# Moving a row copy, splitting the first loads and placing the decay products elsewhere in a linear-attention and mixture-of-experts kernel

## The chip, the cores and the metric

The kernel runs on one core of a Trainium2 chip. The metric is the device time of one execution in microseconds. TensorE (PE in the profile) multiplies, VectorE (DVE), ScalarE (ACT) and GpSimd (POOL) work beside it, and SyncE (SP) issues most of the transfers. POOL and ACT have transfer queues of their own. Engines meet only at semaphores, and each engine takes its instructions strictly in order.

## The reference

The input is layer-normalised once; the output is the input plus an attention branch plus an expert branch.

```
xn  = layernorm(x)                            # x: 1024 tokens x 256
q, k, v = split(xn @ w_qkv);  q, k = elu(.)+1
decay = sigmoid(decay_param)                  # one value for each of 16 heads
kv_t = decay*kv_(t-1) + k_t*v_t;  ks_t = decay*ks_(t-1) + k_t
attn = (q * kv / max(sum_d(q * ks), 1e-6)) @ w_out
e = argmax(xn @ router_w.T);  gate = sigmoid(max logit)
routed = (silu(g) * u) @ w_down[e],  [g, u] = (xn*gate) @ w_gate_up[e]   # 8 experts, top 1
shared = (silu(g') * u') @ shared_down, [g', u'] = xn @ shared_gate_up
out = x + attn + routed + shared
```

## The kernel before

**Tiles.** The 1024 tokens are eight tiles of 128 (`NT`), in two halves of four (`TH` = 4). The work is written out by hand: one list of instructions for each engine, with waits on semaphores between them.

**Start.** SP issues two loads of x with two tiles each, the k part of w_qkv, and, once the second load of x has landed, the v part, the other two loads of x and the q part. ACT issues the small loads of the router and of `decay_param`. PE runs 14 matmuls on constants (L985) in this time, then transposes the router (L989). DVE takes the statistics of the first four tiles (`statistics`, L600), then aggregates all four (L604). ACT takes the root (L451), DVE makes 1/root more exact (L613 to L618) and normalises three tiles (L620); ACT normalises the fourth (L439). PE transposes them (L855), ACT rounds the result to `xT_hi` (L444), and DVE forms the rest, `xT_lo` (`x_lo`, L626), from which the third pair of matmuls of the first projection tile reads (`hi_lo`, L914). The second half follows the same way. `root_eps` is a square root of a constant (L449), which brings the table of square roots into ACT before it is wanted.

**Decay.** After the root of the second half, ACT forms exp(-decay_param) (L466). DVE forms 1/(1+that) after the second `normalise` (L692, L693). PE spreads the 16 values over 128 partitions with two small products (L1006) between projection tiles 6 and 7, and DVE copies the result to `decay` (L733) late in the projection. The scans over tokens read `decay`.

**Middle.** PE runs 12 projection tiles (`qkv_tile`, in PSUM banks 0 to 3 in turn), the router, and seven of the eight shared gate/up tiles. DVE, ACT and POOL place each token in a row of `sorted_rows` in HBM, grouped by expert in tiles of 144 rows.

**Expert tiles.** Eight tiles (t = 0 to 7 here), one for each expert. On PE a tile is: the gate/up products of half 0 (16 matmuls, L1040), the transposes that bring the result of tile t-1 back to rows (`transpose_back`, L979), the gate/up products of half 1, the transposes of the input of tile t+1 (L971), and the down products (L1054), of which the first 8 read the half-0 result of DVE and the last 8 the half-1 result. For each half ACT takes the silu (L541) and DVE multiplies (L793, `hr`). DVE also copies the transposed rows of tile t-1 from PSUM to the one buffer `yrow` (`rows_copy`, L788), and POOL stores `yrow` to `sorted_rows` (L418). Before the copy DVE waits until PE has transposed and until the store before has landed, as `yrow` is one buffer:

```
def rows_copy(t):
    dve.wait_ge(s_yback, t + 1)
    dve.wait_ge(s_ystore, 16 * t + 16)
    V.tensor_copy(yrow[...], ps[0:HS, 7, :]).then_inc(s_yrow, 1)
```

PE in turn waits in `transpose_back(t + 1)` of the next tile for that copy (`s_yrow`), as the rows lie in one PSUM bank. SP refills the expert weights, 1 MB (`gu`, L339) after the gate/up products of a tile and 0.5 MB (`dn`, L341) after its down products, for the expert two further on.

**End.** A ninth `rows_copy` and store (L420) bring the last tile home. When all stores have landed, POOL gathers the eight token tiles (L427). Meanwhile PE runs the last shared tile, the shared down products and the attention output into eight PSUM banks. DVE adds the gathered rows (L834) and the PSUM result (L838); in its order the sum with tile i-4 from PSUM stands behind the sum with gathered tile i. SP stores each finished tile (L359).

Of the kernel before, what the change touches and what calls it, by code (L numbers as in the profile page):

```python
# [13 lines left out]
P = 128  # L14
# [9 lines left out]
def build(nc, x, w_qkv, w_out, decay_param, router_w, w_gate_up, w_down, shared_gate_up, shared_down, out):  # L24
# [23 lines left out]
    with ExitStack() as ctx:  # L48
# [12 lines left out]
        root_eps = sb("root_eps", [P, 1], F32)  # L61
        head_of = sb("head_of", [P, KC, HEADS], F32)
# [116 lines left out]
        s_x = [sem(f"s_x{n}") for n in range(2 * NH)]  # L179
# [113 lines left out]
        def _(sp):  # L293
            def x_load(n):
                two = slice(2 * n, 2 * n + 2)
                sp.dma_start(x_sb[:, two, :], x_rows[:, two, :]).then_inc(s_x[n], 16)
# [5 lines left out]
            x_load(0)  # L302
            x_load(1)
            w_load(1, s_wk)
            sp.wait_ge(s_x[1], 16)
# [127 lines left out]
        def _(act):  # L433
# [11 lines left out]

            act.dma_start(router[:, :], router_w).then_inc(s_router, 16)
            act.dma_start(dec_in[:, :], decay_param.rearrange("(h o) -> h o", o=1)).then_inc(s_dec, 16)
# [17 lines left out]
            act.wait_ge(s_dec, 16)  # L465
            A(dec_e[:, :], dec_in[:, :], ACT.Exp, scale=-1.0).then_inc(s_dece, 1)  # L466
# [112 lines left out]
        def _(dve):  # L579
# [16 lines left out]
            def statistics(i):  # L596

                if i % 2 == 0:
                    dve.wait_ge(s_x[i // 2], 16)
                return V.bn_stats(bn[:, i, :], x_sb[:, i, :])  # L600

            def variances(n):
                for i in range(n * TH, (n + 1) * TH):
                    ins = V.bn_aggr(mv[:, i, :], bn[:, i, :])  # L604
# [66 lines left out]
            for i in range(TH):  # L671
                ins = statistics(i)
            link(ins)
            variances(0)
            normalise(0)
            dve.wait_ge(s_whk, 1)
# [3 lines left out]
            x_lo(0)  # L680
            dve.wait_ge(s_rhi, 1)
# [7 lines left out]
            variances(1)  # L689
            normalise(1)  # L690
            dve.wait_ge(s_dece, 1)
            link(V.tensor_scalar(dec_1[:, :], dec_e[:, :], 1.0, None, ALU.add))  # L692
            V.reciprocal(dec_h[:, :], dec_1[:, :]).then_inc(s_dech, 1)  # L693
# [19 lines left out]
            for a in range(2 * NH):  # L713
# [14 lines left out]
                if a == KC:  # L728
# [3 lines left out]
                    dve.wait_ge(s_decp, 1)  # L732
                    V.tensor_copy(decay[:, :], ps[:, 7, 256:256 + KC]).then_inc(s_decay, 1)  # L733
# [56 lines left out]
            def expert_tile(t):  # L790
                for h in range(2):
# [3 lines left out]
                    if h == 0:  # L795
                        rows_copy(t)
# [44 lines left out]
        def _(pe):  # L841
# [46 lines left out]
            def qkv_tile(t):  # L888
# [7 lines left out]
                if t:  # L896
                    pe.wait_ge(s_xlo, 2 * n + 2)
                if t >= 4:
# [92 lines left out]
            transpose_tokens(0)  # L991
            for t in range(3):
# [121 lines left out]
```

## Time and profile before

| | |
|---|---|
| median of 3 runs | 133.34 us (132.67 to 134.13) |
| the profiled execution | 133.63 us |
| its span, first to last instruction | 132.0 us |
| granted TensorE clock | 1.00 of full |
| PE busy | 125.1 us (95%) |
| DVE, ACT, POOL busy | 79.1, 52.7, 30.9 us |
| chain that ended last | PE 58%, DMA 26%, DVE 7%, ACT 3%, issue 3% |

The span is what the traces show; the execution's time has 1.6 us more around it. The page gives shares over the whole span, the timeline the start and length of single instructions, the windows the sums of a stretch, and the chain what released what.

### The profile page before, as it was taken

What the parts mean: (1) busy time and instruction counts of PE and PEld (TensorE: products, weight loads), DVE (VectorE), ACT (ScalarE), POOL (GpSimd) and SP (SyncE); (2) the same over time, 40 slices, a digit from 0 to 9 for tenths busy, and PEclk for the clock granted to TensorE, in tenths of its full rate; (3) what the DMA queues carried; (4) which work ended last, traced back from release to release, by engine and by line L of the source; (5) the groups of instructions that cost most, each with busy time, mean ns of one, the idle gap of its engine ahead of it and who ended that gap; (6) DMA issues with size and microseconds to landing.
All of it is one profiled execution on the core that took longest, in us unless ns stands there. A gap on an engine that the chain in (4) does not pass through costs nothing.

```text
span 132.0 us, 2426 instructions
## 1 busy us (share of the span) xinstructions
PE 125.1 (95%) x830; PEld 108.3 (82%) x830; DVE 79.1 (60%) x161; ACT 52.7 (40%) x104; POOL 30.9 (23%) x55
## 2 busy tenths in 40 slices
PE   4989989999999999999999999999798999999992
PEld 1247757788888885999999988999697997999991
DVE  0699886989999998455286447401917512413472
ACT  3265796869965956422222221313252223100000
POOL 7704000027786000020202002020202021177600
DMA  2684999999942101029899999999992120123364
GB/s 81 210 267 103 307 354 211 236 376 406 409 181 104 45 0 50 20 60 310 266 296 281 370 394 337 352 349 360 307 353 78 45 69 28 45 82 97 102 195 168
DMA packets 20052, 27.40 MB, mean 208 GB/s; under 512 B 1336, under 2 KB 16864, under 8 KB 20040
## 3 DMA queue, kind: packets, MB, share of 16 engines
q1 hardware_dynamic: 14152, 21.43, 50.2%
q0 software_dynamic: 1408, 3.58, 8.5%
q10 hardware_dynamic: 4480, 2.24, 5.8%
q8 instruction: 7, 0.11, 0.3%
q14 instruction: 5, 0.04, 0.1%
HBM read 19.90 MB, written 7.34 MB: 206 GB/s over the span
## 4 chain that ended last, share of the span: by engine, by line
PE 58%; DMA 26%; DVE 7%; issue 3%; ACT 3%; ACTq 0%; POOLq 0%; DVEq 0%
DMA sorted_rows<-yrow 19%; PE ps L288 10%; PE ps L290 10%; PE ps L289 10%; PE ps L1040 6%; DMA den<-den_rows 5%; PE ps L908 5%; PE ps L1054 4%; PE ps L921 4%; PE ps L914 4%; DMA x_sb<-in_L_attn_x_dram 2%; DVE yrow L788 2%; ACT xT_hi L444 1%; DVE bn L600 1%; PE ps L855 1%
## 5 line engine op out<-in xcount | busy, mean ns | idle before, releaser
L1040 PE MATMUL ps<-xgT,gu 128*128 128x144 f32 x256 | 34.2, 287 | 0.1
L1040 PEld LDWEIGHTS ps<-xgT,gu 128*128 128x128 f32 x256 | 32.4, 190 | 0.7 <-issue 0.5
L1054 PE MATMUL ps<-wqkv,dn 128*128 128x144 f32 x128 | 18.2, 292 | 1.5 <-DVE wqkv L793 1.5
L418 POOL DMA_DIRECT2D sorted_rows<-yrow x8 | 5.6, 699 | 59.6 <-DVE yrow L788 59.6
L1054 PEld LDWEIGHTS ps<-wqkv,dn 128*128 128x128 f32 x128 | 16.3, 190 | 2.2 <-DVE wqkv L793 2.2
L793 DVE TENSOR_TENSOR wqkv<-rz,ps 128x288 f32<-128x288 f32 x16 | 7.2, 451 | 17.4 <-ACT rz L541 17.4
L541 ACT ACTIVATE rz<-ps 128x288 f32<-128x288 f32 x16 | 6.6, 410 | 26.4 <-PE ps L1040 26.4
L288 PE MATMUL ps<-xT_hi,sgu_hi 128*128 128x512 f32 x32 | 12.8, 399 | 0.0
L289 PE MATMUL ps<-xT_lo,sgu_hi 128*128 128x512 f32 x32 | 12.5, 391 | 0.0
L290 PE MATMUL ps<-xT_hi,sgu_lo 128*128 128x512 f32 x32 | 12.5, 390 | 0.0
L788 DVE COPY yrow<-ps 72x512 f32<-72x512 f32 x9 | 6.1, 683 | 10.1 <-DMA sorted_rows<-yrow 7.4
L410 POOL DMA_INDIRECT sorted_rows<-xn,slot_row x8 | 9.8, 1231 | 3.7 <-ACT xn L475 2.1
L544 ACT ACTIVATE yT<-ps 128x288 f32<-128x288 f32 x8 | 3.3, 410 | 14.8 <-PE ps L1054 14.8
L289 PE MATMUL ps<-wqkv_lo,hT_hi 128*128 128x256 f32 x32 | 9.1, 283 | 0.0
L288 PE MATMUL ps<-wqkv_hi,hT_hi 128*128 128x256 f32 x32 | 9.1, 283 | 0.0
L290 PE MATMUL ps<-wqkv_hi,hT_lo 128*128 128x256 f32 x32 | 9.0, 281 | 0.0
L908 PE MATMUL ps<-xT_hi,wqkv_hi 128*128 128x512 f32 x24 | 8.2, 419 | 0.7 <-DVE ksum L716 0.4
L427 POOL DMA_INDIRECT q_sb<-sorted_rows,slot_row x8 | 7.7, 964 | 4.9 <-POOLq L423 2.7
L834 DVE TENSOR_TENSOR x_sb<-x_sb,q_sb 128x256 f32<-128x256 f32 x8 | 3.4, 424 | 7.4 <-DMA q_sb<-sorted_rows,slot_row 7.4
L921 PE MATMUL ps<-xT_hi,wqkv_lo 128*128 128x512 f32 x24 | 7.6, 397 | 0.0
L914 PE MATMUL ps<-xT_lo,wqkv_hi 128*128 128x512 f32 x24 | 7.5, 396 | 0.0
L985 PE MATMUL ps<-ones 128*128 128x512 bf16 x14 | 5.5, 495 | 1.8 <-POOL ones L367 1.8
(153 smaller groups left out, 227.7 us busy)
## 6 DMA issues: line engine op xcount, KB each, us to landing
gu<-in_L_ffn_w_gate_up_dram SPq DMA_DIRECT2D x8, 1024.0 KB, 7.5
dn<-in_L_ffn_w_down_dram SPq DMA_DIRECT2D x8, 512.0 KB, 8.4
sorted_rows<-zeros SPq DMA_DIRECT2D x1, 2592.0 KB, 16.6
sorted_rows<-yrow POOLq DMA_DIRECT2D x10, 144.0 KB, 4.8
wqkv<-sorted_rows SPq DMA_DIRECT2D x10, 144.0 KB
x_sb<-in_L_attn_x_dram SPq DMA_DIRECT2D x4, 256.0 KB, 3.2
sgu<-_ffn_shared_gate_up_dram SPq DMA_DIRECT2D x1, 1024.0 KB, 6.1
rden_rows<-rden ACTq DMA_DIRECT2D x1, 1024.0 KB, 14.0
```

The costliest lines, as they stand in the source:

```text
L288: nc.tensor.matmul(o, w_hi, m_hi, start=start, stop=False)
L289: nc.tensor.matmul(o, w_hi, m_lo, start=False, stop=False)
L290: return nc.tensor.matmul(o, w_lo, m_hi, start=False, stop=stop)
L410: pool.indirect_dma_start(sorted_rows, bass.IndirectOffsetOnAxis(ap=slot_row[:, i:i + 1], axis=0), xn[:, i, :], None).then_inc(s_scatter, 16)
L427: pool.indirect_dma_start(y_tok[:, i, :], None, sorted_rows, bass.IndirectOffsetOnAxis(ap=slot_row[:, i:i + 1], axis=0)).then_inc(s_gather ...
L788: V.tensor_copy(yrow[:, :, :].rearrange("p j d -> p (j d)"), ps[0:HS, 7, :]).then_inc(s_yrow, 1)
L793: V.tensor_tensor(hr[:, 2 * h:2 * h + 2, :].rearrange("p f s -> p (f s)"), act_sb[:, h, 0:2 * SLOTS], ps[:, 2 * h + 1, 0:2 * SLOTS], ALU.m ...
L908: mm(o, wqkv_hi[:, kc, cols], xT_hi[:, kc, rows], start=(kc == 0), stop=False)
L914: ins = mm(o, wqkv_hi[:, kc, cols], xT_lo[:, kc, rows], start=False, stop=last and kc == KC - 1)
L921: ins = mm(o, wqkv_lo[:, kc, cols], xT_hi[:, kc, rows], start=False, stop=last and kc == KC - 1)
L1040: ins = mm(ps[:, 2 * h + u, (f % 2) * SLOTS:(f % 2 + 1) * SLOTS], gu[p][:, kc, col:col + P], xgT[:, kc, :], start=(kc == 0), stop=(kc == K ...
L1054: ins = mm(ps[:, 5 + c, 0:SLOTS], dn[p][:, f, c * P:(c + 1) * P], hr[:, f, :], start=(f == 0), stop=(f == FC - 1))
```

## The change

Three edits go together.

1. In an expert tile DVE does `rows_copy(t)` after both products L793 instead of between them. There is still one buffer `yrow`.
2. The first four tiles of x come in four loads of one tile, tiles 0 and 2 from SP, tiles 1 and 3 from ACT's queue, with a semaphore for each; `decay_param` is loaded between ACT's two and the router after them. DVE waits for each tile and aggregates a tile's statistics one tile later.
3. exp(-decay_param) becomes ACT's first activation, ahead of `root_eps`. A new `exp_eps` (an exp of a constant) stands where the exp stood. DVE's two decay operations come right after the first `normalise`, PE's two small products right after the first transposes (into bank 3), the copy to `decay` after the first `x_lo`. Projection tile 3 waits for that copy.

```diff
-            x_load(0)
-            x_load(1)
+            for i in range(0, TH, 2):
+                sp.dma_start(x_sb[:, i, :], x_rows[:, i, :]).then_inc(s_xt[i], 16)
             w_load(1, s_wk)
-            sp.wait_ge(s_x[1], 16)
+            sp.wait_ge(s_xt[TH - 2], 16)
+            sp.wait_ge(s_xt[TH - 1], 16)
...
+            act.dma_start(x_sb[:, 1, :], x_rows[:, 1, :]).then_inc(s_xt[1], 16)
+            act.dma_start(dec_in[:, :], decay_param.rearrange("(h o) -> h o", o=1)).then_inc(s_dec, 16)
+            act.dma_start(x_sb[:, 3, :], x_rows[:, 3, :]).then_inc(s_xt[3], 16)
             act.dma_start(router[:, :], router_w).then_inc(s_router, 16)
-            act.dma_start(dec_in[:, :], decay_param.rearrange("(h o) -> h o", o=1)).then_inc(s_dec, 16)
+            act.wait_ge(s_dec, 16)
+            A(dec_e[:, :], dec_in[:, :], ACT.Exp, scale=-1.0).then_inc(s_dece, 1)
             act.wait_ge(s_const, 1)
             A(root_eps[:, :], eps[:, :], ACT.Sqrt)
...
-            act.wait_ge(s_dec, 16)
-            A(dec_e[:, :], dec_in[:, :], ACT.Exp, scale=-1.0).then_inc(s_dece, 1)
+            A(exp_eps[:, :], eps[:, :], ACT.Exp)
...
             for i in range(TH):
-                ins = statistics(i)
-            link(ins)
-            variances(0)
+                here = mark(statistics(i))
+                if i:
+                    need(last)
+                    aggregate(i - 1)
+                last = here
+            need(last)
+            variances(0, [TH - 1])
             normalise(0)
+            dve.wait_ge(s_dece, 1)
+            link(V.tensor_scalar(dec_1[:, :], dec_e[:, :], 1.0, None, ALU.add))
+            V.reciprocal(dec_h[:, :], dec_1[:, :]).then_inc(s_dech, 1)
...
             x_lo(0)
+            dve.wait_ge(s_decp, 1)
+            V.tensor_copy(decay[:, :], ps[:, 3, 0:KC]).then_inc(s_decay, 1)
...
             normalise(1)
-            dve.wait_ge(s_dece, 1)
-            link(V.tensor_scalar(dec_1[:, :], dec_e[:, :], 1.0, None, ALU.add))
-            V.reciprocal(dec_h[:, :], dec_1[:, :]).then_inc(s_dech, 1)
...
-                    dve.wait_ge(s_decp, 1)
-                    V.tensor_copy(decay[:, :], ps[:, 7, 256:256 + KC]).then_inc(s_decay, 1)
...
-                    if h == 0:
-                        rows_copy(t)
+                rows_copy(t)
...
+                if t == 3:
+                    pe.wait_ge(s_decay, 1)
...
             transpose_tokens(0)
+            pe.wait_ge(s_dech, 1)
+            for c in range(KC):
+                ins = mm(ps[:, 3, c:c + 1], spread[:, c, :], dec_h[:, :], start=True, stop=True)
+            ins.then_inc(s_decp, 1)
...
             ranks()
-            pe.wait_ge(s_dech, 1)
-            for c in range(KC):
-                ins = mm(ps[:, 7, 256 + c:257 + c], spread[:, c, :], dec_h[:, :], start=True, stop=True)
-            ins.then_inc(s_decp, 1)
```

## Rows read from the trace of the kernel before

**Rows 1.** The page, busy time of each engine and its share of the span.

```profile
PE 125.1 (95%) x830; PEld 108.3 (82%) x830; DVE 79.1 (60%) x161; ACT 52.7 (40%) x104; POOL 30.9 (23%) x55
```

**Rows 2.** Windows, one expert tile each (1, 3, 5, 6): length, then busy us by engine.

```profile
59.33:65.95 6.62, 6.62 (x58) 6.61 (x57) 2.59 (x4) 1.53 (x4) 0.72 (x1) 1.00 0.89 288
...
72.69:80.27 7.58, 7.21 (x57) 6.72 (x57) 3.97 (x6) 1.65 (x5) 0.68 (x1) 1.00 1.08 371
...
87.01:94.70 7.69, 6.89 (x58) 6.66 (x57) 2.64 (x5) 1.53 (x4) 0.68 (x1) 1.00 1.02 331
94.70:102.08 7.38, 6.90 (x59) 6.68 (x58) 3.78 (x6) 3.31 (x6) 0.69 (x1) 1.00 0.68 246
```

**Rows 3.** Timeline of expert tiles 1 and 5: start, length, instruction, [idle before <-releaser].

```profile
61.29 0.60 PE L979 MATMUL ps<-ident,yT 128*72 128x128 f32 x4
...
62.31 0.68 DVE L788 COPY yrow<-ps 72x512 f32<-72x512 f32 x1
...
64.33 0.46 DVE L793 TENSOR_TENSOR wqkv<-rz,ps 128x288 f32<-128x288 f32 x1 [1.35 <-ACT rz L541]
...
92.52 0.69 DVE L788 COPY yrow<-ps 72x512 f32<-72x512 f32 x1 [2.45 <-DMA sorted_rows<-yrow]
...
93.62 0.76 PE L1054 MATMUL ps<-wqkv,dn 128*128 128x144 f32 x4 [0.80 <-DVE wqkv L793]
```

**Rows 4.** The chain that ended last: row stores 2 to 5, from issue to landing.

```profile
70.56 7.13 DMA sorted_rows<-yrow
...
79.20 5.53 DMA sorted_rows<-yrow
...
86.24 6.18 DMA sorted_rows<-yrow
...
93.94 5.86 DMA sorted_rows<-yrow
```

**Rows 5.** DMA issues at 57.16, 71.55 and 106.47 us; last column: us to landing.

```profile
sorted_rows<-yrow POOLq DMA_DIRECT2D x1, 144.0 KB, 3.0
...
gu<-in_L_ffn_w_gate_up_dram SPq DMA_DIRECT2D x1, 1024.0 KB, 8.5
...
sorted_rows<-yrow POOLq DMA_DIRECT2D x1, 144.0 KB, 2.8
```

**Rows 6.** Timeline of the end: ninth copy, first gather, last sums, last output store.

```profile
110.19 0.69 DVE L788 COPY yrow<-ps 72x512 f32<-72x512 f32 x1 [2.65 <-PE ps L979]
...
115.01 1.04 POOL L427 DMA_INDIRECT q_sb<-sorted_rows,slot_row  x1 [2.73 <-POOLq L423]
...
126.76 0.43 DVE L834 TENSOR_TENSOR x_sb<-x_sb,q_sb 128x256 f32<-128x256 f32 x1 [0.49 <-DMA q_sb<-sorted_rows,slot_row]
127.10 0.74 DVE L838 TENSOR_TENSOR x_sb<-x_sb,ps 128x256 f32<-128x256 f32 x2
...
129.44 0.42 DVE L838 TENSOR_TENSOR x_sb<-x_sb,ps 128x256 f32<-128x256 f32 x1 [0.29 <-PE ps L290]
...
129.89 0.33 SPq L359 DMA_DIRECT2D out_dram<-x_sb  x1
```

**Rows 7.** Timeline of the start: ACT's second load, table load, root_eps, first root.

```profile
1.60 0.34 ACTq L447 DMA_DIRECT2D dec_in<-_L_attn_decay_param_dram  x1
...
1.98 1.28 ACT L449 ACT_TABLE_LOAD   x1 [1.98 <-issue]
...
3.27 0.20 ACT L449 ACTIVATE root_eps<-eps 128x1 f32<-128x1 f32 x1
...
5.97 0.30 ACT L451 ACTIVATE sd<-mv,eps 128x4 f32<-128x4 f32 x1 [2.50 <-DVE mv L604]
```

**Rows 8.** Timeline: PE's wait in projection tile 0; DVE's second decay operation.

```profile
10.73 0.19 PEld L914 LDWEIGHTS ps<-xT_lo,wqkv_hi 128*128 128x128 f32 x1 [0.17 <-DVE xT_lo L626]
...
14.83 0.15 DVE L693 RECIPROCAL dec_h<-dec 16x1 f32<-16x1 f32 x1
```

**Rows 9.** The chain that ended last: PE's small decay products (start, us).

```profile
23.85 0.53 PE ps L1006 x4
```

More of the change, by code:

```diff
@@ L61, in build @@
         root_eps = sb("root_eps", [P, 1], F32)
+        exp_eps = sb("exp_eps", [P, 1], F32)
         head_of = sb("head_of", [P, KC, HEADS], F32)
@@ L176, in build @@
         count_ps = ps[:, ROUTE, 192:192 + NT * E]
-        s_x = [sem(f"s_x{n}") for n in range(2 * NH)]
+        s_xt = [sem(f"s_xt{i}") for i in range(TH)]
+        s_x = [sem(f"s_x{n}") for n in range(TH // 2, 2 * NH)]
         s_router = sem("s_router")
@@ L295, in x_load @@
                 two = slice(2 * n, 2 * n + 2)
-                sp.dma_start(x_sb[:, two, :], x_rows[:, two, :]).then_inc(s_x[n], 16)
+                sp.dma_start(x_sb[:, two, :], x_rows[:, two, :]).then_inc(s_x[n - TH // 2], 16)
             def w_load(j, s_w):
@@ L596, in statistics, with aggregate, variances @@
             def statistics(i):
-                if i % 2 == 0:
-                    dve.wait_ge(s_x[i // 2], 16)
+                if i < TH:
+                    dve.wait_ge(s_xt[i], 16)
+                elif i % 2 == 0:
+                    dve.wait_ge(s_x[(i - TH) // 2], 16)
                 return V.bn_stats(bn[:, i, :], x_sb[:, i, :])
-            def variances(n):
-                for i in range(n * TH, (n + 1) * TH):
-                    ins = V.bn_aggr(mv[:, i, :], bn[:, i, :])
+            def aggregate(i):
+                return V.bn_aggr(mv[:, i, :], bn[:, i, :])
+            def variances(n, tiles):
+                for i in tiles:
+                    ins = aggregate(i)
                 ins.then_inc(s_var, 1)
@@ L688, in _ @@
             link(ins)
-            variances(1)
+            variances(1, range(TH, NT))
             normalise(1)
-            dve.wait_ge(s_dece, 1)
-            link(V.tensor_scalar(dec_1[:, :], dec_e[:, :], 1.0, None, ALU.add))
-            V.reciprocal(dec_h[:, :], dec_1[:, :]).then_inc(s_dech, 1)
             dve.wait_ge(s_wlk, 1)
```

## The prediction

> **What bounds the kernel now.** I read the page first: PE is busy for 95% of the span [rows 1]. So there is little idle PE time to win, and the question is where PE waits. The chain of work next: between projection and the last sum it runs through PE, except in the expert stage, where it runs through the stores of `yrow` [rows 4]. That is a warning and not yet a price, since a chain names what came last, not by how much. The windows, cut at the start of each expert tile, give the price: an undisturbed tile takes 6.62 us, tiles 3, 5 and 6 take 7.58, 7.69 and 7.38 [rows 2], which is 0.96 + 1.07 + 0.76 = 2.79 us over. The timeline of tile 5 shows how: DVE stands 2.45 us before the copy, waiting for the store, and the half-1 product behind it comes late, so that PE waits 0.80 us between its two halves of down products [rows 3]. The start and the end are the other places where PE isn't the only engine on the path.
>
> **Edit 1, the copy behind both products.** In this order the store no longer stands in front of the half-1 product. The loop itself stays: copy, 1.42 us until the store is issued (92.52 to 93.94), landing, some 0.1 us, next copy [rows 3, 4]. Its period is 1.42 + landing + 0.1; the four landings of 7.13, 5.53, 6.18 and 5.86 us [rows 4] give 8.65, 7.05, 7.70 and 7.38, mean 7.69, more than a tile's 6.62. What changes is the slack. The half-1 product starts 5.00 us into a tile (59.33 to 64.33), so an undelayed copy starts at 5.0 + 0.37 = 5.37 us instead of 62.31 - 59.33 = 2.98 [rows 2, 3]; 0.37 is the distance from product to copy that tile 1 shows. The next to need it is PE's transpose back, 1.96 us into the next tile (61.29) [rows 3]; the copy must start 0.76 us before it, at 7.8 us. So the loop may fall behind by 2.4 us before PE waits, but it starts 2.4 us later and is bound by the store from tile 0 on, not from tile 2.
>
> The first copy comes at 52.7 + 5.37 = 58.1 (tile 0 begins one tile of 6.62 before 59.33). With p the mean of six periods (stores 0 to 5) the seventh copy starts at 58.1 + 6p, tile 7's transpose back 0.76 later, and the stage ends 6.62 - 1.96 = 4.66 after that: 58.1 + 6p + 5.4. It ended at 108.6, one undisturbed tile after 102.08 [rows 2]. PE's own limit: in tile 3 the wait hides another one. The 1 MB refill issued at 71.55 lands after 8.5 us, at 80.05 [rows 5], and tile 4 begins at 80.27, the end of tile 3 [rows 2]. So tile 3's 0.96 stays, and at most 1.07 + 0.76 = 1.83 us can go.
>
> What are the periods? Store 0 now follows the refill of `gu` instead of preceding it; preceding it, it landed in 3.0 us [rows 5]. The nearest row for a store behind a refill with little else in flight is 5.86 (period 7.38) [rows 4]; the bounds are 3.0 and 7.13. I take five periods of 7.5 and a sixth of 6.5, because by then the refills run out (after them a store landed in 2.8 us [rows 5]): 58.1 + 37.5 + 6.5 + 5.4 = 107.5, a gain of **1.1 us**. With 7.38 throughout it is 107.8 (0.8 gained); with 7.4 five times and 6.5 it is 107.0, close to the limit of 1.83; with 7.69 throughout it is 109.6, a loss of 1.0.
>
> Then the end, where the price is firmer. Before, the ninth copy (110.19) waited for PE's transposes [rows 6] because store 7 had been issued at 106.47 and had landed after 2.8 us, at 109.3 [rows 5]. Copy 7 now comes 2.4 us later within its tile, so store 7 is issued at 108.9 and lands at 111.7 on the old scale: the ninth copy is 1.5 us later against PE. POOL's eight gathers stand behind the ninth store, the first at 115.01, and move with it. The sum with the last gathered tile, at 126.76, moves to 128.3. Behind it in DVE's queue stand the PSUM sums of tiles 3 to 7. Two of them took 0.74 us with 0.42 for one, so they follow each other by 0.32 [rows 6]: the last starts near 128.3 + 0.35 + 4 x 0.33 = 130.0 instead of 129.44, 0.55 later. Their output stores are then issued back to back by SP at 0.33 us each [rows 6] and about 0.1 between, 0.43 x 4 after a first at 129.1: the last at 130.8 instead of 129.89. I take **0.9 us lost**, bounds 0.5 and 1.5. DVE's `hidden(LAST)` also stands behind the ninth copy; it moves by 0.3 us, and PE has two shared-down tiles ahead of its need.
>
> Other work behind the moved copy on DVE, the scans, `sdn_lo` and the attention products, moves by up to 2.4 us. Only in tile 4 does it get near a product (q times kv and `wout_lo`, 3 us after copy 3); worth 0 to 0.5 us, which the range holds.
>
> **Edit 2, four loads.** Statistics start when the first 256 KB have landed, and the root follows at 5.97 [rows 7]. Half the size for tile 0 and aggregation between the tiles would let the root start some 0.2 to 0.4 us earlier: three of the four aggregations leave the path. But ACT is in the way. Its four issues (0.34 us for the small one [rows 7], about 0.5 for each of x) end near 2.8; a table load of 1.28 us follows and ends at 4.1. The exp waits for `decay_param`, issued at 1.6 and now between loads of x: between 4.2 and 4.6. After it comes the second table load of 1.28, and `root_eps`, 0.2 [rows 7]: the root can run at 5.9 to 6.2. Before, one table load ended at 3.26, long before it was needed. So the earlier statistics meet a busier ACT: **0.1 us lost**, bounds 0.3 gained and 0.3 lost. SP's wait for tile 3 moves the v weights and the later x loads by up to 0.4 us. They are covered, since the v part is first rounded after `x_hi(0)`.
>
> The Trainium skill ("ScalarE: Activation LUTs", the section on table sets and the one on what a table load costs) says to batch activations by set and not to alternate exp and sqrt, and prices each switch at about 1.28 us of load plus 1.38 us of drain. That speaks against this edit, which adds one switch. The trace agrees on the load; the drain doesn't show, as `root_eps` starts at 3.27, right at the end of the load [rows 7]. By the page's 2.66 us a switch the root would stand near 2.8 + 2.66 + 0.2 + 2.66 + 0.2 = 8.5, an estimate from that page.
>
> **Edit 3, the decay products.** They leave PE's dense stretch, where they cost 0.53 us [rows 9]: a gain of 0.5, since tile 7's banks are free by then. They enter between the first transposes and projection tile 0, where PE waits for ACT's `xT_hi`. No row bounds that but the two extremes, 0 (all under the wait) and 0.53 (none); I take 0.15, near the first, as PE has nothing else there. DVE's two operations of 0.15 [rows 8] enter before `w_lo` and `x_lo`. That is no idle gap on DVE: PE already waits 0.17 us for `xT_lo` in tile 0 [rows 8], so their 0.3 us goes straight through. The two delays overlap, since tile 0 waits for both in turn: 0.3 in all. DVE's copy of 0.15 before the router's remainder has slack until the router's products. Leaving the second `normalise` they free nothing that PE waits for. Sum: 0.5 - 0.3 = **0.2 us gained**, bounds 0.5 gained and 0.1 lost.
>
> **The sum.** On the profiled execution: 133.63 - 1.1 + 0.9 + 0.1 - 0.2 = 133.3. The median of the runs is 0.3 below that execution, so 133.34 - 0.3 = 133.0. A measurement of this kernel can tell about 1%, 1.3 us, from no change.
>
> **The rivals.**
>
> A. The store loop is never late (chance 0.22). If stores behind the refill land in 3 to 5 us, like store 0, then p is under 7.1, PE loses only the refill wait, and 1.83 goes. Less traffic ahead of the refills could bring these forward too and free the 0.96 of tile 3, 2.8 in all. With 0.6 at the end instead of 0.9 and the start on the good side (0.3 gained in place of 0.1 lost) that is 133.34 - 1.83 - 0.2 - 0.3 + 0.6 = 131.6, down to 130.7. For it: 3.0 us in [rows 5]. Against it: every store in [rows 4] that was issued near a refill took 5.5 us or more.
>
> B. The loop overtakes PE (0.18). One mechanism: the transpose back of tile t+1 waits for copy t, which waits for store t-1. It decides above p = (108.6 - 63.5)/6 = 7.52. At the mean of before, 7.69, the stage is 1.0 us longer, and with the end the time is 133.34 + 1.0 + 0.9 + 0.1 - 0.2 = 135.1. For it: two of the four periods before are above 7.52, and the loop is now bound two tiles earlier, with the 1 MB reciprocal store still in flight. Against it: that traffic was what made 7.13.
>
> C. Table loads hold the root (0.06). If the load for the exp started only after `decay_param` has landed (4.3), two loads would end at 7.1 and the root stand 1.2 us later: 133.0 + 1.2 = 134.2. The page of the Trainium skill named above would make it 2.5 and 135.5, an estimate. For it: nothing in [rows 7] orders load and wait. Against it: the load before began at 1.98, right after the issues.
>
> **How the numbers follow.** My forecast, a small gain inside the noise, has 0.54; its own range is 132.1 to 134.2. A reaches down to 130.7, B up to 135.1 and beyond. A range of 131.4 to 135.1 leaves out about 0.2. Faster by over 1% means under 132.0: most of A, 0.21. Slower means over 134.7: B, part of C and a bad end, 0.22. The rest is 0.57.
>
> **What would show each step.** Tile windows: 3 stays near 7.5, 5 and 6 fall to 6.6 to 7.0. PE's waits move from the down products to L979, if any. Copies stand 5.4 to 7.8 us into their tiles. The ninth copy is released by the store, not by PE; the gathers start 1.5 us later against PE's last shared tile; the last output stores go out back to back. At the start two table loads precede the first root, which stands within 0.3 us of 5.97. The gap before L914 in tile 0 grows by 0.2 to 0.3. The prediction is wrong if the mean period lies outside 7.1 to 7.6, or if ACT's start order costs more than its loads.

## The result, and the profile after

The changed kernel takes 137.5 us (median of 6 runs, 136.6 to 139.1); the kernel before took 133.0 us beside it (6 runs, 132.3 to 134.1). The ratio is 1.033, interval 1.026 to 1.040: by it the change is 4.4 us slower, where 0.3 us faster was forecast and the range ended at 135.1. Ratios, here and below, are of executions within about 1.5% of the fastest of their kernel, so that edit 3 alone rests on 4 of 12 executions, the buffers with edit 3 on 6 of 12 and the attention run on 3 of 6, and the profiles of edit 3 alone and of the attention run are of executions that their ratios leave out.

The profiled execution of the changed kernel took 137.72 us with a span of 136.1, 4.1 more than before. Its granted clock was 0.993 over the whole; it was 1.00 up to the end of the expert stage and 0.96 behind it, where PE's last product is nevertheless where it was (below). So the clock doesn't explain the loss.

The windows, cut at the starts of expert tiles 1, 3, 5 and 6 as in [rows 2] (length, busy us by engine, clock, DMA share, GB/s):

```profile
59.36:65.98 6.62, 6.62 (x58) 6.61 (x57) 2.58 (x4) 1.53 (x4) 0.77 (x1) 1.00 0.86 289
72.61:80.27 7.66, 6.85 (x58) 6.64 (x57) 3.81 (x5) 1.53 (x4) 0.69 (x1) 1.00 1.04 353
87.82:95.95 8.13, 6.81 (x58) 6.60 (x57) 1.50 (x3) 1.53 (x4) 0.69 (x1) 1.00 1.00 312
95.95:104.26 8.31, 7.02 (x58) 6.67 (x57) 3.77 (x5) 3.42 (x6) 0.68 (x1) 1.00 0.70 237
```

The stage begins at 52.74, 0.03 later than before. Tile 5 takes 8.13 for 7.69 and tile 6 8.31 for 7.38; tile 4 takes 7.55 where it took 6.74. The last tile begins at 104.26 and, at 6.62, the stage ends at 110.9 instead of 108.7. So 2.2 us of the 4.1 are lost inside the stage, and 1.9 behind it.

The chain that ended last (start, us, piece) says through what. Before, it ran through four stores [rows 4]; now it enters the store loop at the first copy and leaves it only after the fifth store, through two other engines:

```profile
58.11 0.69 DVE yrow L803
...
59.58 6.64 DMA sorted_rows<-yrow
...
67.75 6.95 DMA sorted_rows<-yrow
...
76.21 5.48 DMA sorted_rows<-yrow
...
83.20 7.22 DMA sorted_rows<-yrow
...
91.93 5.29 DMA sorted_rows<-yrow
...
97.92 2.36 DVE kvsum L834 x2
100.30 1.06 ACT att_hi L577
101.36 0.31 ACT rz L547
101.69 0.47 DVE wqkv L808
```

From 58.11 to the copy at 97.31 there is no slack: the loop sets the pace of five tiles. The timeline shows where PE feels it:

```profile
75.54 0.63 PE L995 MATMUL ps<-ident,yT 128*72 128x128 f32 x4 [0.81 <-DVE yrow L803]
...
85.75 2.23 PE L1070 MATMUL ps<-wqkv,dn 128*128 128x144 f32 x16 [0.39 <-DVE wqkv L808]
...
90.51 0.69 DVE L803 COPY yrow<-ps 72x512 f32<-72x512 f32 x1 [4.45 <-DMA sorted_rows<-yrow]
...
91.26 0.63 PE L995 MATMUL ps<-ident,yT 128*72 128x128 f32 x4 [1.32 <-DVE yrow L803]
...
97.31 0.69 DVE L803 COPY yrow<-ps 72x512 f32<-72x512 f32 x1 [2.53 <-DMA sorted_rows<-yrow]
...
99.17 2.19 ACT L577 ACTIVATE att_hi<-kvsum 128x1024 fp32r<-128x1024 f32 x2 [2.60 <-DVE kvsum L834]
...
102.20 2.23 PE L1070 MATMUL ps<-wqkv,dn 128*128 128x144 f32 x16 [1.29 <-DVE wqkv L808]
```

PE no longer waits between its two halves of down products for a product caught behind the copy [rows 3]; it waits in the transposes back for the copy itself (L995). Two waits have another reason: work that stands on DVE behind the late copy. In tile 4 the scan's product and `wout_lo` stand between copy 3 and the expert products, and PE waits 0.39 us ahead of its down products. In tile 6 it waits 1.29 us: the two attention products (L834) stand on DVE behind copy 5, ACT's `att_hi` (L577) waits for them, and ACT's silu of tile 6 stands behind `att_hi`.

The end, against [rows 6]:

```profile
113.77 0.69 DVE L803 COPY yrow<-ps 72x512 f32<-72x512 f32 x1 [3.46 <-DMA sorted_rows<-yrow]
...
118.63 1.04 POOL L430 DMA_INDIRECT q_sb<-sorted_rows,slot_row  x1 [2.76 <-POOLq L426]
...
131.22 0.42 DVE L848 TENSOR_TENSOR x_sb<-x_sb,q_sb 128x256 f32<-128x256 f32 x1 [1.39 <-DMA q_sb<-sorted_rows,slot_row]
...
131.89 1.40 DVE L852 TENSOR_TENSOR x_sb<-x_sb,ps 128x256 f32<-128x256 f32 x4
...
132.00 2.29 SPq L362 DMA_DIRECT2D out_dram<-x_sb  x5
```

Counted from the end of the stage, the ninth copy is 1.4 us later (2.9 for 1.5), the first gather 1.4 (7.75 for 6.3), the sum with the last gathered tile 2.3 (20.3 for 18.1), and SP's last store ends 1.9 later (23.4 for 21.5). PE's last product is where it was, 20.4 us behind the stage, in both. Before, the last sum still waited for PE, 0.29 us [rows 6]; now the last sums stand behind the last gather.

The start, against [rows 7, 8]:

```profile
1.88 0.44 ACTq L451 DMA_DIRECT2D x_sb<-in_L_attn_x_dram  x1
...
3.00 1.28 ACT L454 ACT_TABLE_LOAD   x1 [3.00 <-issue]
4.30 0.20 ACT L454 ACTIVATE dec_e<-dec_in 16x1 f32<-16x1 f32 x1
4.51 1.28 ACT L456 ACT_TABLE_LOAD   x1
5.81 0.20 ACT L456 ACTIVATE root_eps<-eps 128x1 f32<-128x1 f32 x1
6.38 0.30 ACT L458 ACTIVATE sd<-mv,eps 128x4 f32<-128x4 f32 x1 [0.37 <-DVE mv L611]
...
5.70 0.43 DVE L608 BATCH_NORM_STATS2 bn<-x_sb 128x6 f32<-128x256 f32 x1 [1.04 <-DMA x_sb<-in_L_attn_x_dram]
...
11.37 0.19 PEld L930 LDWEIGHTS ps<-xT_lo,wqkv_hi 128*128 128x128 f32 x1 [0.40 <-DVE xT_lo L637]
```

The root is 0.41 us late, and what released it was not the second table load (over at 5.79, `root_eps` over at 6.01) but the statistics of tile 3, whose load was the last of the four to be issued, by ACT at 1.88. With DVE's two decay operations in front as well, PE comes 0.64 us late to its transposes of the second half; the dense stretch gives 0.53 back, as PE's small products have left it. So the stage begins only 0.03 us later.

### The profile page after: what moved, and what is told of

Its sections match the earlier page's. It is cut to its first block, busy times and chain, and to the rows that moved or that the text cites. A ratio compares the mean times of both kernels' runs of the same rounds, so it can differ in the third digit from the quotient of the medians.

```text
span 136.1 us, 2432 instructions
## 1 busy us (share of the span) xinstructions
PE 125.5 (92%) x830; PEld 108.1 (79%) x830; DVE 78.6 (58%) x161; ACT 54.3 (40%) x106; POOL 32.1 (24%) x55
## 4 chain that ended last, share of the span: by engine, by line
PE 43%; DMA 30%; issue 8%; DVE 7%; POOL 5%; ACT 3%; DVEq 1%; POOLq 1%
DMA sorted_rows<-yrow 27%; PE ps L1056 6%; PE ps L290 5%; PE ps L291 5%; PE ps L292 5%; PE ps L1001 5%; POOL q_sb L430 4%; PE ps L924 4%; PE ps L930 4%; PE ps L937 4%; DVE yrow L803 4%; DMA q_sb<-sorted_rows,slot_row 3%; DVE kvsum L834 2%; PE ps L1070 2%; PE ps L869 1%
## 5 line engine op out<-in xcount | busy, mean ns | idle before, releaser
L1070 PE MATMUL ps<-wqkv,dn 128*128 128x144 f32 x128 | 17.5, 290 | 1.7 <-DVE wqkv L808 1.7
L413 POOL DMA_INDIRECT sorted_rows<-xn,slot_row x8 | 11.3, 1407 | 2.8 <-issue 1.8
L1001 PE MATMUL ps<-ones 128*128 128x512 bf16 x14 | 6.2, 627 | 1.8 <-POOL ones L370 1.8
L995 PE MATMUL ps<-ident,yT 128*72 128x128 f32 x36 | 5.5, 276 | 2.3 <-DVE yrow L803 2.1
```

What stands on the lines that cost most here:

```text
L413: pool.indirect_dma_start(sorted_rows, bass.IndirectOffsetOnAxis(ap=slot_row[:, i:i + 1], axis=0), xn[:, i, :], None).then_inc(s_scatter, 16)
L1001: mm(ps[:, 0, :], ones[:, :], ones[:, :].unsqueeze(1).broadcast_to([P, 4, P]), start=True, stop=True)
L1070: ins = mm(ps[:, 5 + c, 0:SLOTS], dn[p][:, f, c * P:(c + 1) * P], hr[:, f, :], start=(f == 0), stop=(f == FC - 1))
```

## The experiments

Each was timed in turns with the kernel before on the same chip. They ran in four sessions on four chips, in which the kernel before took 134.5 to 135.2 us (medians), against 133.0 when the change was measured; the whole change wasn't timed again. So 1% is 1.35 us, and differences between rows of different sessions are less sure than the rows.

| | ratio to the kernel before | interval |
|---|---|---|
| whole change | 1.033 | 1.026 to 1.040 |
| edit 1 alone | 1.017 | 1.007 to 1.027 |
| edits 2 and 3 | 1.011 | 1.003 to 1.018 |
| edit 2 alone | 1.011 | 1.005 to 1.018 |
| edit 3 alone | 0.996 | 0.990 to 1.002 |
| change, four row buffers | 1.001 | 0.997 to 1.006 |
| before, four row buffers | 0.995 | 0.992 to 0.999 |
| before once more (control) | 1.003 | 0.999 to 1.008 |
| change, attention products first | 1.011 | 1.004 to 1.019 |
| change, no refills | 0.994 | 0.990 to 0.998 |
| before, no refills | 0.984 | 0.979 to 0.989 |
| before, buffers and edit 3 | 0.996 | 0.992 to 1.001 |
| edit 2 alone, tile 3 first | 1.002 | 0.998 to 1.006 |
| copy behind in the last tile alone | 1.010 | 1.004 to 1.017 |
| change, tile 3 first | 1.039 | 1.032 to 1.046 |
| before, buffers, edit 2 with tile 3 first | 0.989 | 0.984 to 0.995 |

**Which edit loses.** Edit 1 alone:

```
-                    if h == 0:
-                        rows_copy(t)
+                rows_copy(t)
```

> The kernel before with edit 1 alone: the row copy behind both products, the start untouched. Theory S (the loop of copy, store and next copy overtakes PE, and the copy drags what stands behind it on DVE): nearly all of the loss is here, 136.5 to 137.5 us; tiles 3 to 6 take 7.5 to 8.3 us, the mean of the six copy periods is near 7.7, the gathers start 3.5 us later than before. Rival T (the new start, or the lower granted clock, makes the loss): 133 to 133.5 us.

and the other two without it (the copy back between the products):

> The changed kernel with the row copy back between the two products, so edits 2 and 3 alone. Theory S: 133.0 us within 0.7, the expert stage begins within 0.1 us of the kernel before because the root that is 0.4 us later and the decay products taken out of the dense stretch cancel; tiles 3, 5 and 6 over 7.3 us again with PE waiting in the down products. Rival T: 136 to 137 us.

They give 1.7% and 1.1%, together 2.8% against the 3.3% of the whole, which the intervals allow. Edit 1 alone lost somewhat less than was expected (136.5 to 137.5 us would be 2.4 to 3.1%), and edits 2 and 3 lost where both theories were wrong: S had no loss, T had all of it. Nor does their profile show the 1.1%: the stage begins at 52.86 and ends at 108.8, against 52.71 and 108.7 before.

In the profile of edit 1 alone copies 0 to 6 run from 57.9 to 102.3, a mean period of 7.40, and the last tile begins at 101.87 (102.08 before). The ninth copy now waits for the store, and in tile 6 PE waits by way of the attention products as in the whole change:

```profile
99.80 2.23 PE L1053 MATMUL ps<-wqkv,dn 128*128 128x144 f32 x16 [1.08 <-DVE wqkv L793]
...
111.15 0.69 DVE L788 COPY yrow<-ps 72x512 f32<-72x512 f32 x1 [3.23 <-DMA sorted_rows<-yrow]
```

At 7.40 the forecast's formula has the stage end at 57.9 + 44.4 + 5.4 = 107.7, a stage 0.8 us shorter than before; it ends at 108.5 and is as long as before (56.0 us). Copy 6 was 0.75 us early for tile 7, so it wasn't the loop that set the start of the last tile here, but the wait in tile 6. The period differs from execution to execution (7.40 here, 7.70 in the change), and even at 7.40 the stage gains nothing. This profile (135.7 us) was the second shortest of four runs; one profile isn't the median.

**Is it the single buffer?** The row buffer was replaced by four (two in turn for tiles 0 to 6, one for tile 7, one for the last copy; seven transfers of 4 bytes ahead of the stage keep a semaphore's count):

```
-        yrow = sb("yrow", [HS, 2, D], F32)
+        yrow = [sb(f"yrow{b}", [HS, 2, D], F32) for b in range(4)]
...
+                    if t >= 2:
+                        dve.wait_ge(s_yalt[b], 16 * (t // 2))
```

In the changed kernel:

> The changed kernel with four row buffers: the first seven tiles alternate between two, the eighth and the ninth copy have one each, so a copy waits for the store two tiles before or for none. Seven one-word transfers from POOL ahead of the stage keep the semaphore counts. Theory S: no copy waits for a store, no PE wait before the transposes back, tile windows 6.6 to 6.8 except at most 0.4 to 0.9 where a refill of weights lands late, the ninth copy is released by PE again, 130.3 to 131.5 us. Rival D (the delay comes from DVE work standing behind a copy that is in any case 2.4 us later in its tile): tiles 4 and 6 stay at 7.3 us or more, 132.5 us or more.

and in the kernel before:

> The kernel before (copy between the products, old start) with the same four row buffers. Theory S: its three long tiles lose their waits, except what the late refill leaves in tile 3: 130.5 to 131.5 us, within 0.6 of the same buffers with the copy behind. If the refills of weights were the real bound, tiles 3 and 5 would stay above 7.2 and the time above 132.

In both no copy waits for a store any more, and the last tiles begin at 100.75 and 100.17. The loss of the change falls from 3.3% to 0.1%: what edit 1 loses needs the single buffer. In neither does PE wait for a product of DVE in the stage, so rival D falls as well. Both runs were expected some 2% faster than the kernel before and weren't: the second gains half a per cent, less than the 1.8 us that its waits for the copy seemed to be worth. PE waits for loads instead (timeline, before with four buffers):

```profile
77.58 0.47 PE L992 MATMUL ps<-ident,wqkv 72*128 72x72 f32 x4 [0.68 <-DMA wqkv<-sorted_rows]
```

and the refill of `gu` issued at 71.36 lands after 8.6 us, at 79.96, ahead of a tile 4 that begins at 80.22: the wait that [rows 2, 5] had shown for tile 3.

**Is it the refills?** SP's refills were left out in both orders, so that experts 2 to 7 work with the weights of experts 0 and 1 and the routed part of the result is another one:

```
-                sp.wait_ge(s_gup, 2 * done)
-                sp.dma_start(gu[p][:, :, :], gu_dram[e + 2]).then_inc(s_gu[p], 16)
-                sp.wait_ge(s_down, done)
-                sp.dma_start(dn[p][:, :, :], dn_dram[e + 2]).then_inc(s_dn[p], 16)
```

> The changed kernel without the refills of the expert weights (experts 2 to 7 work with the weights of experts 0 and 1; that part of the result is another one). Theory (the landing of the 144 KB stores under 1.5 MB refills is what makes the loop late): stores land in 2.6 to 3.5 us, a period is about 4.5 us and never binds, no copy before the eighth waits for a store, all tiles take 6.62 us, the stage ends near 105.7. Only the end stays: the ninth copy waits for store 7 (about 108.6) and stands 1.3 us later than in the kernel before without refills. Together with 0.1 to 0.3 at the start the time is 1.0 to 1.6 us above that kernel. Rival (the late copy itself costs in the stage, whatever the transfers do): tiles above 6.62 us remain.

> The kernel before without the refills of the expert weights, left out as in the run beside it. All eight tiles take 6.62 us, no copy waits for its store, the stage ends near 105.7 instead of 108.6 to 109.0, and the time is about 2.9 us under the kernel before, ratio 0.975 to 0.985. If the ratio stays above 0.99, the transfers weren't what held the stage.

All tiles of both kernels take 6.62 us. The windows of tile 5, first of the change, then of before, with a DMA share of 0.15 and 0.17 instead of 1.0:

```profile
85.81:92.44 6.63, 6.63 (x59) 6.62 (x58) 2.08 (x4) 1.54 (x4) 0.69 (x1) 1.00 0.15 44
```

```profile
85.58:92.20 6.62, 6.62 (x58) 6.61 (x57) 2.67 (x5) 1.53 (x4) 0.68 (x1) 1.00 0.17 47
```

The refills cost the kernel before 1.6% (2.2 us) and the changed one 3.9% (1.033 against 0.994, of different sessions; 5.2 us). About two thirds of the change's loss hang on them. The rival, that the late copy costs in the stage whatever the transfers do, falls: with copies that wait for no store the work behind them holds up nothing either. What is left, 1.1% or 1.4 us, is put down to the end and the start (0.23 us between the stage's starts, 52.70 and 52.47); the end is seen in the last copy of each, the change first:

```profile
108.40 0.69 DVE L799 COPY yrow<-ps 72x512 f32<-72x512 f32 x1 [3.29 <-DMA sorted_rows<-yrow]
```

```profile
106.93 0.69 DVE L784 COPY yrow<-ps 72x512 f32<-72x512 f32 x1 [2.65 <-PE ps L975]
```

**The end by itself.** The copy stands behind both products in the last tile alone:

```
-                    if h == 0:
+                    if h == 0 and isinstance(t, int):
                         rows_copy(t)
+                if not isinstance(t, int):
+                    rows_copy(t)
```

(the last tile runs in a loop with a counter in a register; the others have t as a number).

> The kernel before with the row copy behind both products in the last expert tile alone, all others as before. It measures the forecast's end term by itself. Forecast: copy 7 comes 2.4 us later, store 7 is issued near 108.9 to 109.3 and lands 2.8 us later, the ninth copy is released by that store 1.5 us later than by PE before, the eight gathers move with it, the last five sums go back to back; 0.5 to 1.5 us longer, ratio 1.004 to 1.011. Rival (the end has slack, and the whole loss is in the stage): ratio 1.000 to 1.003, and the gathers later by the same 1.5 us without the last store moving.

It costs 1.4 us, 0.5 to 2.3. Its timeline has the forecast's mechanism: the copy 5.37 us into the tile, the ninth released by the store, the gather behind it.

```profile
107.45 0.68 DVE L788 COPY yrow<-ps 72x512 f32<-72x512 f32 x1
111.50 0.69 DVE L788 COPY yrow<-ps 72x512 f32<-72x512 f32 x1 [3.37 <-DMA sorted_rows<-yrow]
...
116.33 1.04 POOL L427 DMA_INDIRECT q_sb<-sorted_rows,slot_row  x1 [2.73 <-POOLq L423]
```

Counted from the stage's end the first gather comes 1.3 us later than in the control below, and SP's last store ends 0.8 later. The rival of a free end falls.

**The attention products.** In the changed kernel the copy of tile 5 was put behind them:

```
-                rows_copy(t)
+                if not (isinstance(t, int) and t == 5):
+                    rows_copy(t)
...
                 V.tensor_tensor(kvsum[:, c, :], kvsum[:, c, :], rspread[:, c, :], ALU.mult).then_inc(s_att, 1)
+            rows_copy(5)
```

> The changed kernel with one line moved: the row copy of tile 5 stands behind the attention products on DVE, so that these don't wait for store 4. Theory 1 (a second path of the late copy: DVE's attention product, ACT's att_hi ahead of the silu of tile 6, the product of tile 6, PE's down products): PE's wait of 1.3 us in tile 6 goes, but copy 5 is later by the products' time of about 1 us and store 5 with it, so copy 6 and 7 may make PE wait instead; tile 6 is 0.5 to 1.4 us shorter, the time 0.3 to 1.2 us less than the changed kernel, ratio to the kernel before 1.022 to 1.030. Theory 2 (only the store loop counts): tile 6's gain is lost again in tile 7, which waits for copy 6, and the ratio stays at 1.032 as with the whole change.

The ratio, 1.011, rests on three of six runs, and all six lay between 135.9 and 144.2 us with a median of 137.9, which is 1.021 of the median beside it; it settles nothing. The profile (138.6 us) shows the exchange: PE's wait for the down products is gone, and as the products wait for a load of the reciprocals, the copy behind them is late and PE waits for it 1.96 us.

```profile
96.66 2.36 DVE L835 TENSOR_TENSOR kvsum<-kvsum,ksum 128x1024 f32<-128x1024 f32 x2 [3.26 <-DMA ksum<-rden_rows]
...
99.67 0.63 PE L997 MATMUL ps<-ident,yT 128*72 128x128 f32 x4 [1.96 <-DVE yrow L803]
```

The last tile begins at about the same time as in the change. The side chain itself shows in three other profiles, with 1.29 us in the change, 1.29 in the change with tile 3 first and 1.08 in edit 1 alone; what it alone is worth in the timed runs stays open.

**The control.**

> The kernel before, unchanged, as one more run beside the others. Its profile tells whether the longer end seen in the four earlier experiments (DVE's first PSUM sum some 3.1 us after the fifth gather sum, 1.1 in the profile of before) comes from their edits or not. If not: the same gap of about 3.1 us here, stores of yrow landing in 5.5 to 7.1 us in the middle of the stage, tile starts as in the profile of before to 0.3 us. Ratio 1.00.

It is needed, as the end of every experiment's profile has a stall of PE's own that the profiles of before and after lack:

```profile
126.85 0.38 PE L289 MATMUL ps<-wqkv_lo,att_hi 128*128 128x256 f32 x1 [0.42 <-issue]
```

The control has it too (its last product is 21.6 us behind the stage's end, 20.4 before), so it belongs to no edit. Control and before also differ by 0.24 us at the stage's start and, counted from the stage's end, by 1.6 at the sum with the last gathered tile and 1.7 at SP's last store (23.2 for 21.5). This is the grain of one profile, and the 1.9 us that the profile after has over before at its end (23.4) are hardly above it: the end is sized by the run on the last tile, not by a pair of profiles.

**Edits 2 and 3 apart.**

> The kernel before with edit 2 alone (four loads of x on two queues, exp ahead of the square root). My theory after the result: the loads share the DMA engines with the k weights, tile 3 lands near 5.6 us, the root stands about 0.4 us later (6.3 to 6.5), the expert stage begins 0.3 to 0.6 us later and the time is 0.3 to 0.6 us longer, ratio 1.002 to 1.005. Rival (the forecast's case C): the second table load holds the root; then the root starts right at the end of that load and not at DVE's variances.

> The kernel before with edit 3 alone (decay products behind the first transposes). My theory: DVE's two decay operations delay the first projection tile by 0.15 to 0.35 us, the four products leave the dense stretch and give 0.53 back, so the expert stage begins 0.15 to 0.35 us earlier than with the kernel before, and the time is 0.1 to 0.4 us shorter, ratio 0.997 to 1.000. Rival: the four products come on top of PE's wait for the split of x, the gain is eaten at the start, and the stage begins where it did, ratio 1.000.

The expectation of the first describes it wrongly: in its edit the exp stays behind the second root, and its profile has one table load ahead of the first root (3.00 to 4.28). So this run couldn't meet rival C, and the exp belongs to edit 3. Edit 2 alone loses 1.1%, more than the theory's 0.6 us. Its profile has two delays: tile 3 of x (0.28 us of waiting at 5.44, the root at 6.12, released by DVE's statistics), and, later, the fifth and sixth tile, which SP issues only when tile 3 has landed. DVE waits for them and the split of x behind them comes late; PE's weight loads then wait 0.37 and 0.41 for `xT_lo` (0.19, once, in the control):

```profile
9.45 0.75 DVE L606 BATCH_NORM_STATS2 bn<-x_sb 128x6 f32<-128x256 f32 x2 [0.46 <-DMA x_sb<-in_L_attn_x_dram]
```

Edit 3 alone can't be told from no change (over all its executions the median is 135.3 against 135.1 us); the gain of 0.2 forecast for it fits, but isn't shown. Its profile holds two things that the forecast didn't have there. The second table load holds the root: the exp waits for `decay_param` until 4.48, the statistics are ready at 5.69, and the root starts 0.41 us later, right behind the load and `root_eps`.

```profile
4.70 1.28 ACT L452 ACT_TABLE_LOAD   x1
...
6.10 0.28 ACT L454 ACTIVATE sd<-mv,eps 128x4 f32<-128x4 f32 x1
```

The profile of the buffers with edit 3 has the same with 0.16 us. And GpSimd rounds one part of the weights while DVE rounds another. First the profile of edit 3 alone, then the control:

```profile
11.11 1.71 DVE L632 TENSOR_TENSOR wqkv_lo<-wqkv,wqkv_hi 128x512 fp32r<-128x512 f32 x1
...
10.98 1.28 POOL L402 TENSOR_TENSOR wqkv_lo<-wqkv,wqkv_hi 128x512 fp32r<-128x512 f32 x1 [5.28 <-ACT wqkv_hi L465]
```

```profile
10.89 0.68 DVE L630 TENSOR_TENSOR wqkv_lo<-wqkv,wqkv_hi 128x512 fp32r<-128x512 f32 x1
...
11.46 1.29 POOL L401 TENSOR_TENSOR wqkv_lo<-wqkv,wqkv_hi 128x512 fp32r<-128x512 f32 x1 [5.76 <-ACT wqkv_hi L462]
```

Where GpSimd starts first, DVE's operation lasts 1.03 us longer, to 0.56 after GpSimd's end; PE's weight load waits 0.78 us for it and the product 0.35, and the stage begins at 53.48, 0.5 later than in the control. Edit 3 puts DVE's operation some 0.3 us later behind the root and so can make it lose that race. It doesn't always: with the buffers DVE was first (10.86 against 10.99), and the stage began at 52.17, 0.35 earlier than with the buffers alone, which is the gain that was forecast, in one profile of each. In the change GpSimd is late as well (11.97, DVE 11.40). So what one edit does to the start can't be read off the profile of another combination.

**Why tile 3 is late.** Edit 2 alone, with one thing changed:

```
             act.dma_start(x_sb[:, 1, :], x_rows[:, 1, :]).then_inc(s_xt[1], 16)
+            act.dma_start(x_sb[:, 3, :], x_rows[:, 3, :]).then_inc(s_xt[3], 16)
             act.dma_start(dec_in[:, :], ...).then_inc(s_dec, 16)
-            act.dma_start(x_sb[:, 3, :], x_rows[:, 3, :]).then_inc(s_xt[3], 16)
```

> Edit 2 alone with one thing changed: ACT issues tile 3 of x right behind tile 1, and decay_param after it. Theory (tile 3 is late because it is issued 0.9 us after the others, beside the k weights): tile 3 lands about 0.4 us earlier, near 5.0, the root stands at 5.7 to 6.0 instead of 6.12 to 6.5, and SP's wait ends as much earlier, so the v weights and the later tiles of x come 0.4 us earlier. Rival (four half-sized loads beside the k weights are slower however they are ordered): tile 3 lands at 5.4 to 5.7 as before, and nothing moves.

```profile
4.67 0.39 DVE L606 BATCH_NORM_STATS2 bn<-x_sb 128x6 f32<-128x256 f32 x1
...
5.31 0.30 ACT L455 ACTIVATE sd<-mv,eps 128x4 f32<-128x4 f32 x1 [0.83 <-DVE mv L609]
```

Issued 0.47 us earlier, tile 3 is there at least 0.8 us earlier (by 4.67 instead of 5.44), the root stands at 5.31, earlier than was expected, and the ratio falls from 1.011 to 1.002, in another session and with intervals that just touch. But a root 0.3 to 0.9 us ahead of those of the old order (5.64 to 6.17) gains nothing: the router's transposes, first in PE's order, come at 7.65 (7.24 before, 7.63 in the control), and the stage begins at 52.60, within the 52.4 to 52.95 of the old order.

Then the whole change in the new order:

> The whole change with tile 3 of x issued by ACT ahead of decay_param. If the order of the loads is what edit 2 lost, as the run on edit 2 alone says (1.011 against 1.002), the ratio falls from 1.033 to about 1.024 (1.018 to 1.028). Here the exp stands ahead of the square root: decay_param lands 0.5 us later, near 4.8, so the exp ends at 5.0, the second table load near 6.3 and the root can't start before 6.4, as late as in the change. Rival: the table loads then hold the root, the root stays at 6.3 to 6.5 and the ratio stays at 1.03.

Here the rival held, and the ratio was 1.039. `decay_param` comes last, and in the change the exp stands ahead of the root:

```profile
5.16 0.20 ACT L454 ACTIVATE dec_e<-dec_in 16x1 f32<-16x1 f32 x1 [0.89 <-DMA dec_in<-_L_attn_decay_param_dram]
5.38 1.28 ACT L456 ACT_TABLE_LOAD   x1
6.67 0.20 ACT L456 ACTIVATE root_eps<-eps 128x1 f32<-128x1 f32 x1
6.78 0.28 ACT L458 ACTIVATE sd<-mv,eps 128x4 f32<-128x4 f32 x1
```

The statistics were ready at 5.3; the root waited 1.5 us for table loads. GpSimd was first again as well (11.66 against DVE's 11.78, which took 1.72), and the stage began at 54.34. This is what the forecast's rival C was about, a root held by table loads, though not in the way it said: the first load runs ahead of the wait for `decay_param` (2.98), and only the second stands behind it. The change itself had escaped by 0.37 us, and edit 3 alone had not. By the Trainium skill ("ScalarE: Activation LUTs", what a table load costs) a switch has 1.38 us of drain besides its load: here load follows exp by 0.02 us and `root_eps` the load by 0.01, so no drain shows.

**A version that beats both.** Buffers with edit 3:

> The kernel before with four row buffers (copy between the products) and edit 3, as a candidate for the fastest. From the two runs alone (0.995 and 0.996, each with an interval of half a per cent) 0.990 to 0.997 if the gains add up. If GpSimd's part of the weight rounding starts ahead of DVE's again, as in the run with edit 3 alone, DVE's operation takes 1.7 us instead of 0.68 and the ratio is 0.995 to 1.00.

0.996, 0.992 to 1.001: no more than the buffers alone. Buffers with edit 2 in the mended order (exp and decay products where they were):

> A candidate for the fastest: the kernel before with four row buffers (copy between the products), and four loads of x with tile 3 issued ahead of decay_param (exp where it was, decay products where they were). Buffers alone gave 0.995, the loads in this order 1.002. 0.992 to 1.000; under 0.995 only if the root, 0.5 us earlier, is worth something.

0.989, interval 0.984 to 0.995: 1.5 us under the kernel before. Its stage begins at 52.22 and its last tile at 99.94. Against buffers alone (0.995) the difference is inside the intervals.

## Why the prediction was wrong

Of the 4.4 us between the 133.3 forecast for the profiled execution and its 137.7, 3.3 are in the expert stage (2.2 lost for 1.1 gained), 1.0 at the end and 0.1 at the start.

**The period was mis-sized, and rival B came in.** The first copy stands at 58.11, as worked out, and tile 3's 0.96 stays, as said. The six periods were put at 44.0 us (five of 7.5, one of 6.5); that is a mean of 7.33; they are 8.21, 8.47, 6.99, 8.73, 6.80 and 7.00, 46.2 in all, a mean of 7.70, where B decides above 7.52 (7.53, as 102.08 + 6.62 is 108.7 and not 108.6). The formula with 46.2 gives 109.7, a loss of 1.0 where 1.1 gained was forecast. The failed step is this choice of the periods: it went by the single store that seemed nearest (5.86) instead of the mean of the four periods in [rows 4], 7.69. That this mean agrees to 0.01 is luck, as edit 1 alone had 7.40. The reason for choosing lower, that the stores now run beside fewer transfers, had no row behind it; the run without refills shows the refills as the cause, and they were as many as before.

**The work behind the moved copy.** For tile 4 "0 to 0.5 us" was right (PE waits 0.39, and waits for copy 4 right after it anyway); that it was the only place was wrong, and this is the second step that failed. The forecast looked at DVE's own products alone. The attention products behind copy 5 release an ACT operation that stands ahead of a silu, and PE waits 1.29 us: the other 1.2 us between 109.7 and 110.9. It isn't a matter of the period alone: in edit 1 alone, with a mean period of 7.40, inside the forecast's own bounds of 7.1 to 7.6, PE waited 1.08 us there, and the stage gained nothing where the formula has 0.8 us. What of this is in the timed runs isn't settled, as the run meant for it exchanged one wait for another.

**The timed runs say the same of edit 1.** Alone it cost 2.3 us (1.0 to 3.7), where 1.1 gained and 0.9 lost had been forecast. With 1.4 for the end by the run on the last tile, about 0.9 are left for the stage, a difference of two uncertain numbers.

**The end.** 0.9 forecast with bounds of 0.5 and 1.5; 1.4 (0.5 to 2.3) by the run on the last tile, 1.9 in the profile after. The mechanism was right in each step: the ninth copy and the gathers 1.4 later (1.5 forecast), five sums and five stores back to back. The size isn't shown to be off, as 0.9 lies inside the interval; in the profile after, 0.9 of the excess is the last gather, which landed after 3.7 us instead of 2.8.

**Edit 2.** 0.1 forecast, 1.5 (0.6 to 2.4) timed, and the blame was wrong. In the change, table loads don't hold the root; tile 3's load does, and the issue order decides it, as the mended order shows. (The forecast counted the exp's table load under edit 2; it comes with edit 3, and there it does hold the root, by 0.41 and 0.16 us in two profiles.) "Covered" for SP's later loads was wrong too: DVE waited 0.46 for them. The profile of edit 2 alone has the stage begin at 53.42 against 52.40 to 52.95 in the old order, 0.5 to 1.0 later; the rest of the timed loss isn't explained, nor are the 1.4 us (0.4 to 2.4) that edits 2 and 3 lose together, whose profile begins the stage within 0.15 us of before.

**Edit 3.** Forecast 0.2 gained; timed 0.4% faster, 0.2% slower to 1.0% faster, so neither right nor wrong. The 0.53 us left the dense stretch as said. The collision with GpSimd was not foreseen, and neither was the root held in this edit by itself.

**Rival A** asked for stores that land in 3 to 5 us; of the six stores of the change that this concerns none did (5.3 to 7.2). **The range** ended at B's price with the stage at the mean of before. It left out the side chain, the end's upper bound and edit 2's cost together, each on the same side.

## What to carry to other kernels

A copy that is held by its own buffer gained nothing here from a better place in the queue: it got slack for one consumer and started the loop later for all; more buffers took the loop away. When the period of such a loop is near the period of the stage, take the mean of the landings that the trace has, not the row that fits the hope, and follow every wait behind the moved instruction through the other engines. Look at a load's place in the issue order (0.47 us of it moved a root by 0.8 us), and run each edit alone: it tells what they hide from each other.

## What the runs showed that was not expected

In the rounding of the weights DVE and GpSimd block each other: DVE's operation took 0.66 to 0.69 us in fifteen profiles and 1.71 and 1.72 in the two where GpSimd's had started 0.13 and 0.12 us before it; where DVE was first, GpSimd's took up to 1.70 for 1.29. The Trainium skill ("SBUF — State Buffer", the section on two separate sides) says that the two share a port pair, and that of a DVE instruction with two inputs in SBUF and a GpSimd one that reads SBUF the one that starts first holds it for the whole instruction. The traces agree: the later one ended 0.56 us (DVE) or 1.16 us (GpSimd) behind the end of the first, nearly its own full length.

A store of 144 KB landed in 2.6 to 3.0 us with little beside it and in 5.3 to 7.2 us beside the refills in the profiles before and after. With four buffers they were 5.1 to 7.3 us, and 4.6 and 3.6 for two late ones.

PE stood still for about 1.2 us in all within its last products in the control, with nothing that the profile names, and the other profiles of experiments have such a stall at 123 to 132 us, while the profiles of before and after have none. It may be a part of why the kernel before took 1.5 to 2.2 us more beside the experiments than beside the change, which no run shows. Its cause is open.
